# Swapping two score matmuls in the diagonal blocks of an attention kernel, and moving a drain call by one block

## The reference, cut to what matters

```python
xn = _layernorm(x, axis=-1)
s = _L0_attn_ref(xn, L0_attn_qkv_weights)        # 16 heads of 64, causal
g = _silu(_L0_ffn_ref(xn, L0_ffn_weight_q, L0_ffn_weight_scale, L0_ffn_bias))
x = x + s * g
# inside the attention, S = 4096, Dh = 64:
k = jnp.transpose(pre_k, (0, 2, 3, 1)).reshape(-1, S, Dh)   # a reshape, not a transpose back
a = jnp.einsum('aib,ajb->aij', q, k) / scale
a = tril * a + NEG_INF * (1.0 - tril)
a = jax.nn.softmax(a, axis=-1)
heads = jnp.einsum('aij,ajb->aib', a, v)
```

## Time and profile before

| | us |
|---|---|
| median of 2 runs | 1567.91 (1566.76 to 1569.05) |
| the profiled execution | 1570.01 |
| its slowest core, first to last instruction (core 6) | 1568.5 |
| its fastest core (core 4) | 1551.1 |

### The profile page before, as it was taken

How to read it: one execution, slowest core, us unless ns; L and a number is a source line. 1 busy time by engine, 2 the same in 40 slices (tenths; PEclk the granted TensorE clock), 3 DMA queues, 4 the chain that set the end, 5 groups by cost and what they waited for, 6 DMA issues and landing times.

```text
span 1568.5 us, 17868 instructions; the slowest of 8 cores (1551.1 to 1568.5 us)
## 1 busy us (share of the span) xinstructions
PE 1122.1 (72%) x5200; PEld 463.8 (30%) x5200; DVE 575.2 (37%) x1086; ACT 719.3 (46%) x905; POOL 302.7 (19%) x412
## 2 busy tenths in 40 slices
PE   0335546446465558998887888888888888888886
PEld 0112212212221124444433333334333333333332
DVE  0484382562735553227336226321722111100000
ACT  0121220211211213455445356557647777788886
POOL 1440330411504541113013023011301000000000
PEclk9967757658576665867887988998899988999998
DMA  7110010100101121112002002000100000000000
GB/s 118 47 34 14 23 32 0 34 21 0 41 14 54 54 61 41 41 54 63 19 28 64 12 27 62 7 21 28 34 8 21 14 14 14 15 27 14 9 13 14
DMA packets 24463, 47.46 MB, mean 30 GB/s; under 512 B 4272, under 2 KB 7472, under 8 KB 24368
## 3 DMA queue, kind: packets, MB, share of 16 engines
q1 hardware_dynamic: 15552, 25.34, 5.5%
q0 software_dynamic: 8816, 20.98, 5.4%
HBM read 40.54 MB, written 8.39 MB: 31 GB/s over the span
## 4 chain that ended last, share of the span: by engine, by line
PE 37%; DVE 24%; ACT 18%; issue 8%; POOL 6%; DMA 5%; DVEq 1%; ACTq 0%; POOLq 0%; SPq 0%
ACT eT L780 16%; PE Oa L794 5%; PE pm L555 4%; PE pm L538 4%; PE Ob L798 4%; PE pm L585 3%; PE sT L735 3%; DMA xst<-x 3%; DVE t_r L433 3%; DVE t_b L437 3%; DMA w8n<-w 2%; PE pm L848 2%; PE pm L852 2%; DVE bnst L240 2%; DVE t_g L430 2%
## 5 line engine op out<-in xcount | busy, mean ns | idle before, releaser
L780 ACT ACTIVATE eT<-sT 128x1024 bf16<-128x1024 f32 (+1 forms) x576 | 548.9, 953 | 260.8 <-PE sT L741 131.0
L794 PE MATMUL Oa<-eT,v_aug 128*65 128x512 bf16 (+1 forms) x576 | 241.6, 420 | 2.6
L798 PE MATMUL Ob<-eT,v_aug 128*65 128x512 bf16 (+1 forms) x576 | 229.5, 403 | 0.0
L735 PE MATMUL sT<-qT,kTa 64*128 64x512 bf16 x448 | 182.7, 417 | 37.2 <-ACT eT L780 35.2
L741 PE MATMUL sT<-qT,kTa 64*128 64x512 bf16 x448 | 185.6, 423 | 0.0
L897 POOL DMA_DIRECT2D out<-outs x32 | 24.3, 758 | 730.3 <-DVE outs L890 639.1
L833 DVE TENSOR_TENSOR wpr<-Oa,gT 64x512 bf16<-64x512 f32 x32 | 21.9, 683 | 363.4 <-PE Ob L798 362.4
L301 PE MATMUL sT<-Wqk,xnK 128*128 128x512 bf16 x256 | 111.1, 613 | 47.3 <-ACT xnK L289 42.8
L735 PEld LDWEIGHTS sT<-qT,kTa 64*128 64x128 bf16 x448 | 40.3, 94 | 224.2 <-issue 221.8
L794 PEld LDWEIGHTS Oa<-eT,v_aug 128*65 128x65 bf16 x576 | 68.1, 118 | 106.2 <-issue 94.1
L585 PE MATMUL pm<-xnq,wqT 128*128 128x512 bf16 x256 | 74.7, 444 | 26.3 <-DVE g1s L590 21.3
(11 more groups left out here) (122 smaller groups left out, 1605.3 us busy)
## 6 DMA issues: line engine op xcount, KB each, us to landing
xst<-x SPq DMA_DIRECT2D x96, 256.0 KB, 2.9
xres<-xr POOLq DMA_DIRECT2D x32, 256.0 KB, 3.6
out<-outs POOLq DMA_DIRECT2D x32, 256.0 KB, 2.8
Wqk<-wq POOLq DMA_DIRECT2D x1, 1024.0 KB, 15.5
Wqk<-wk POOLq DMA_DIRECT2D x1, 1024.0 KB, 24.9
Wv<-wv POOLq DMA_DIRECT2D x1, 1024.0 KB, 30.2
w8n<-w POOLq DMA_DIRECT2D x4, 256.0 KB, 2.6
wscb<-wsc SPq DMA_DIRECT2D x4, 0.5 KB, 5.7
```

The costliest lines, as they stand in the source:

```text
L735: t.matmul(sT[par][:, o:o + w], kTa[0:64, P, 128 * jb:128 * jb + 128], qT[P][0:64, qb + o:qb + o + w], start=True, stop=True), waits=w0)
L780: s.activation(eT[pe3][:].rearrange("p (b n) -> p b n", b=2)[:, :, o:o + w], sT[par][:].rearrange("p (b n) -> p b n", b=2)[:, :, o:o + w], ...
L794: sc.emit("tensor", lambda t: t.matmul(Oa[:, o:o + w], v_aug[:, jb, 65 * hA:65 * hA + 65], eT[pe3][:, o:o + w], start=(jb == 0), stop=(jb ...
L798: c_av = sc.emit("tensor", lambda t: t.matmul(Ob[:, o:o + w], v_aug[:, jb, 65 * hB:65 * hB + 65], eT[pe3][:, 512 + o:512 + o + w], start=( ...
```

## The change

Two edits in `emit_attention_chunk`. The first calls `drain_pre` one block later in pair 0 (`jb == 4c - 1`). The second emits head B's 128-column score matmul (line 757) directly behind head A's (line 748), and both mask matmuls behind them. The same matmuls are issued with the same operands; the waits and the semaphore increments stay on the first and the last of them.

```diff
             for jb in range(njb):
-                if P == 0 and jb == 4 * c - 2:
+                if P == 0 and jb == 4 * c - 1:
                     drain_pre()
@@
                         qT[P][0:64, qb + o:qb + o + 128],
                         start=True, stop=False), waits=w0)
-                    sc.emit("tensor", lambda t, o=o, par=par: t.matmul(
-                        sT[par][:, o:o + 128], idb[:], nmk[:],
-                        start=False, stop=True))
                     sc.emit("tensor", lambda t, P=P, jb=jb, o=o, par=par, qb=qb:
                             t.matmul(
                         sT[par][:, 512 + o:512 + o + 128],
                         kTa[64:128, P, 128 * jb:128 * jb + 128],
                         qT[P][64:128, qb + o:qb + o + 128],
                         start=True, stop=False))
+                    sc.emit("tensor", lambda t, o=o, par=par: t.matmul(
+                        sT[par][:, o:o + 128], idb[:], nmk[:],
+                        start=False, stop=True))
                     c_sc = sc.emit("tensor", lambda t, o=o, par=par: t.matmul(
                         sT[par][:, 512 + o:512 + o + 128], idb[:], nmk[:],
                         start=False, stop=True), inc=None if w > 128 else "pe")
```

## The result

| | before | after |
|---|---|---|
| median of the runs, us | 1567.27 (8 runs) | 1525.74 (9 runs) |
| ratio | | 0.9738 (0.972 to 0.9756) |
| slowest and fastest core of the profiled execution, us | 1568.5, 1551.1 | 1528.4, 1510.0 |

In some executions of any of these kernels one whole die shows a lower granted clock and takes some per cent longer; such runs are left out of the ratios and of the medians of the experiments, and without the one among the 9 the median after is 1525.2 us.

The account below looks back on a forecast made before the run. PE was taken as the bound, in diagonal units even in the last two chunks. The swap's 35.9 us less 5.8 hidden gave 30, the drain nothing: 1570.0 to 1540.0 us profiled, 1538 us as median, range 1532 to 1543.

Parts of the forecast that it names:

- What bounds the diagonal units: In diagonal units the others wait for PE: 1.26 us on PE against 0.81 us of exponential on ACT.
- The drain: The drain call issues nothing at either place, so moving it one block later costs exactly nothing.
- The sum of PE's time: Swap in 128 diagonal units: 99 x 0.26 + 29 x 0.35 = 35.9 us of PE's time.
- The four distances: Starts of matmuls from L748 to L767 in a diagonal unit: 0.64 us before, 0.38 after, 0.26 less at 2.4 GHz.
- The unknown, mask to mask: Distance between the two mask matmuls' starts, not in the trace: taken as 0.06 us, possibly 0.16.
- rival 1: In diagonal units the second mask doesn't start early, distance near 0.16 us; 1550 us, chance 0.09.
- What is hidden: PE's savings absorbed by waits in chunks 0 to 5: 5.8 us, at most 10.5; none in chunks 6 and 7.
- The clock: Shift of time between 2.4 and 1.2 GHz, priced at 0.5 us for each us at the lower level.
- rival 3: Slowest core keeps a better clock pattern in the last chunks: 8 to 12 us more gain, about 1528; chance 0.10.
- The prediction's own sign for this: Forecast wrong if the granted clock of the attention stage moves by more than 0.02.
- Rival 4: Clock takes gain back, since denser units do not fill pauses at pair ends; middle case 1573 us, chance 0.03.
- Rival 2: Chains of DVE, `pm` and ACT absorb all but chunks 6 and 7: 8.3 us gained, 1560; chance 0.07.

Follow-up runs that it names:

- masks_first: Changed kernel with both mask matmuls moved ahead of the two 128-column score matmuls in each diagonal unit; 1515.43 us, ratio 0.9668 to the kernel before.
- fill_c67: Kernel before plus five unused 512-column matmuls in the gating steps of the 8 pairs of chunks 6 and 7; 1556.38 us, ratio 0.9928.
- masks_inside: Changed kernel with diagonal units reordered to score A, mask A, mask B, score B; 1545.05 us, ratio 0.9861 to the kernel before.

## Why the prediction was wrong, point by point

- **What bounds the diagonal units: right.** PE does; ACT's idle time before the exponentials of diagonal units was the reserve. It is nearly used up after the change, which `masks_first` ran into.
- **The drain: right.** Nothing is issued; same lists, ratio 0.9994.
- **The sum of PE's time: right.** 36.0 us were measured in the diagonal units' four matmuls, 35.9 forecast, with 28.4 units at the lower level where 29 were forecast.
- **The four distances: right.** 0.16, 0.07, 0.15 and no distance between the halves; 0.244 to 0.261 us less in each of the four units of a pair against 0.26. The unknown, mask to mask, came out at the end that I took (0.06), and rival 1 (0.16) fell. The Trainium skill's rule that a change of tiling mode drains TensorE (TensorEngine Tiling (Array Packing), Key Properties) agrees with the distances of every order tried.
- **What is hidden: right in size.** 35.9 less 31 is 4.9 us, against 5.8. PE's idle time grew by 8.3 us on the mean core (some of it because the other matmuls got faster too), inside the bound of 10.5: by 2.0 us in chunks 0 and 1 (forecast 1.4), by 6.4 in chunks 2 to 5 (forecast 4.4) and not at all in chunks 6 and 7, as forecast. The single waits were not tested; PE's waits for `xnq` by L485 and for exponentials by L748 came out at 27.0 and 8.3 us on core 0, against 24.9 and 6.5 on core 6 before (the waits of PE in the attention stage):

```profile
PE pt L485 <- DVE xnq L495: 27.0, 10, 4.7
PE sT L748 <- ACT eT L780: 8.3, 18, 1.8
```

```profile
PE pt L485 <- DVE xnq L495: 24.9, 9, 4.8
PE sT L748 <- ACT eT L780: 6.5, 18, 1.3
```

- **The clock: this step failed.** The prediction made it rival 3, an accident of where the low stretches fall, with 0.10, and left it out of the sum: all matmuls outside the diagonal units were taken to cost the same after the change. They took 15.2 us less. The mean core spent 48 us less at 1.2 GHz, and with the waits counted that is worth 11.8 us by the slope. Its price was also about twice too high: 0.5 us for each us at the lower level, from two cores and one chunk; all cores together give 0.245, though in chunks 6 and 7 `fill_c67` found 0.35. With the measured term beside the forecast's own 30.1 the sum would have been 1567.3 - 30.1 - 11.8 = 1525.4 us; nothing in the rows of before told how large that term would be. That rival 3's figure, 8 to 12 us, came out is luck: it was to come from a lucky pattern on the slowest core in the last chunks, and it came on the mean core, about half of it in chunks 0 and 1. The prediction's own sign for this, a granted clock of the stage that moves by more than 0.02, was set too wide: it moved from 0.859 to 0.879.
- **Rival 4: fell.** It argued that denser units do not fill the pauses at the pair ends. They need not: the largest rise was in chunks 0 and 1 (0.70 to 0.78 on core 3), where 32 of the 48 units are diagonal and (1 - 0.70) / 0.5 = 0.6 of the time had been at 1.2 GHz. Its arithmetic was off as well: 2% slower is 31.4 us above the time before, so 61 us to lose, and at 0.5 us each 123 us more at the lower level, not 180.
- **Rival 2: fell.** In chunks 0 to 5 the swap gave 32 us of run time, where this rival left nothing.

What stays open: the exact split. That the swap gave 36.0 us in its own matmuls and 15.2 in the others is counted; that 31 and about 11 are left of them after the waits rests on a line through the profiles, not on a run with the clock fixed. A part of the 48 us is no better clock either: the four matmuls at the lower level got shorter, from 28.4 x 0.88 = 25 to 21.3 x 0.55 = 12 us. And why the new order brings the better clock with it is not shown, as `masks_inside` tells.

## What to carry to other kernels

Read the distance between the starts of neighbouring matmuls, sorted by who stands beside whom: where half-row and full-row matmuls alternate, put like beside like, and expect the next engine (here the exponential on ACT) to take over as the bound before the whole saving is in. In a last unit without a rest, count the changes separately. Where the records show much time at 1.2 GHz, a change to PE's order can come with a second term, the clock: give it a place in the sum and a range, with a price from many cores and not from one pair, and expect that it may also stay away, as in `masks_inside`. Check afterwards whether matmuls that the change leaves alone got faster. And where PE pauses anyway, matmuls that nobody reads can be worth putting there: 160 of them took 24 us off `masks_first` and off the changed kernel, and about 30 off the kernel before.

## What the runs showed of the hardware that I had not expected

- At full clock a change between 64-row and 128-row matmuls of 128 columns costs about 0.10 us (0.16 or 0.15 between starts against 0.06 or 0.07), in either direction, and it makes no difference whether mask or score comes first.
- Two plain matmuls of 128 rows with a weight load each stand 0.06 or 0.07 us apart, with the same weights in both.
- A 64-row matmul on the other half of the rows starts beside one of different width at once (L760 and L767 at 1525.04), and the next on its own half 0.07 us later.
- Five matmuls without use in the pause at each of a chunk's pair ends raised the granted clock of chunk 7 from 0.909 to 0.978 over all cores.
- Orders that differ in nothing but the place of four 128-column matmuls have different clocks: 42.8 us of chunks 0 and 1 at the lower level in one, 66.6 in another.
